# A message-passing kernel: when GpSimd may gather ahead, a step later for the first scatters, and where VectorE adds the biases

## The chip, the cores and the metric

One core of a Trainium2 chip. The metric is the device time of one execution in microseconds (us); lower is better. TensorE is called PE below, VectorE DVE, ScalarE ACT, GpSimd POOL and SyncE SP, as in the profile.

## The reference

25,000 edges, sorted by destination, join rows of `x` (100,000 nodes by 128, f32). Every edge makes a message, a gate weighs it, the messages are added up by destination, and each row of the result is normalised:

```python
src, tgt = (x[row], x[col])
h = jax.nn.relu(concatenate([src, tgt, edge_attr], axis=-1) @ W1 + b1)
msg = h @ W2 + b2
attn_weight = jax.nn.sigmoid(concatenate([msg, conf], axis=-1) @ Wa + ba)
out = segment_sum(msg * attn_weight, col, num_segments=N)
return layernorm(x + out)       # every one of the 100,000 rows
```

## The kernel before

The edges are worked off in 49 **steps** of 512 edges (four columns of 128). Sixteen steps are *near* steps (edges into the first 11,648 nodes, whose sums stay in SBUF in `near`), 33 are *list* steps (the other edges, whose rows are written one by one to `out`). `STEPS` fixes their order: list 0, list 1, near 15, list 2, list 3, near 14, then list 4 to 12 one after another (steps 6 to 14), near 13 (step 15), and from there mostly two list steps and a near one by turns. Beside the steps, 63 **chunks** of 1,408 plain rows of `x` are loaded, normalised and stored, three chunks for every two steps (one **batch**).

In a step k:

- POOL issues indirect DMAs, one for each column: four for the source rows (`gather_src`, into one of `RING` = 4 buffers of `rows_src`) and in a list step four more for the destination rows (`gather_dst`, into a ring of 4 `rows_dst` buffers that counts list steps alone; it waits for `stashed`, four list steps back). It also issues the **scatters** of finished list steps, four a list step, at the steps that `SCATTERS` names. All of these stand in one queue in program order.
- PE turns the three inputs (`turn(k)`: sources, destinations, attributes; each part raises `turned_ps_ready`), ACT copies them out, PE multiplies (`hidden(k)`), ACT applies relu, PE makes the messages (`messages(k)`, raises `msg_ready`).
- DVE adds the biases (`add_bias(k)`: a small `logit` and the raw messages `gated`, L1378 and L1381). ACT makes the gates and scales the messages (`gates(k)`).
- DVE adds the messages up, in a list step with `sum_list` (`acc`, then `stash`), in a near step with `sum_near` after PE placed them. At every even k DVE also runs `batch_scales`: a chain of 11 small dependent instructions (L1167 to L1178) with some normalising rows between them, ahead of it `near_stats` in some batches.

PE works off hidden(k), then placing or turning of sums (`sum_near`, `sum_head`, `turn_sums`), then turn(k+1), then messages(k). ACT works off relu(k), turn(k+1), rows of a chunk, gates(k), more rows. Both queues are in order, as DVE's is. At steps 13, 29 and 46 the PE queue has a `sum_head`, whose result DVE takes near the end of `sum_list` (L1330); a `turn_sums` in the same step (L959) waits until DVE has taken it (L1332), and turn(k+1) stands behind that.

What holds a gather back in the kernel before is `AHEAD` = 2: the gather of step k waits until PE has turned all three inputs of step k-2, although the ring has four buffers. The first scatters (list steps 0 and 1, at step 15) wait for the last plain chunk of their region to be stored and for the first part of `near` (`near_stored[0]`).

Of the kernel before, what the change touches and what calls it, by code (L numbers as in the profile page):

```python
# [14 lines left out]
G = 4  # L15
RING = 4
AHEAD = 2
SLOTS = 6
TRIO = 3
ROWS = 11  # L20
# [34 lines left out]
K = len(STEPS)  # L55
STEP_OF = {at: k for k, at in enumerate(STEPS)}

SCATTERS = {15: (0, 1), 18: (2, 3), 21: (4, 5), 24: (6, 7), 27: (8, 9), 29: (10,),
            32: (11, 12), 35: (13, 14), 38: (15, 16), 41: (17, 18), 44: (19, 20), 46: (21,),
            48: tuple(range(22, 33))}  # L60
STASH_G = 14
# [145 lines left out]
def build(nc, x, src, dstw, attr, conf, W1, b1, W2, b2, Wa, ba, out):  # L207
# [9 lines left out]
    with ExitStack() as ctx:  # L217
        def sb(name, shape, dt=F32):
            return ctx.enter_context(nc.sbuf_tensor(name, shape, dt))
# [4 lines left out]
        def sem(name):  # L224
            return ctx.enter_context(nc.semaphore(name))

        def sems(name, n):
            return [sem(f"{name}{i}") for i in range(n)]
# [45 lines left out]
        near = sb("near", [P, (NB + BEHIND) * F])  # L274
        nodes = sb("nodes", [P, SLOTS, ROWS, F])
        stats = sb("stats", [P, 2, WIDEST, STATS])
# [113 lines left out]
        near_landed = sem("near_landed")  # L390
        x_landed = sems("x_landed", SLOTS)
        turned_ps_ready = sem("turned_ps_ready")
# [19 lines left out]
        scale_free = sem("scale_free")  # L412
        normed = sems("normed", SLOTS)
        near_normed = sem("near_normed")
        stored = sems("stored", SLOTS)
        near_stored = sems("near_stored", len(NEAR_BATCHES))
# [46 lines left out]
        def chunk_parts(c):  # L463
            return REST_P if c == CHUNKS - 1 else P

        def chunk_of(view, c):
            n = chunk_parts(c)
            return view[ND + c * CHUNK:ND + c * CHUNK + n * ROWS].rearrange("(p r) f -> p r f", p=n)
# [15 lines left out]
        def table(t, i):  # L484

            return t[:, i // LG, (i % LG) * G:(i % LG) * G + G]
# [13 lines left out]
        def _(sp):  # L500
# [7 lines left out]
            def load_nodes(c):  # L508
                n = chunk_parts(c)
                sp.dma_start(nodes[0:n, c % SLOTS], chunk_of(x, c)).then_inc(x_landed[c % SLOTS], 16)  # L510

# [52 lines left out]
            def store_nodes(c):  # L564
                u, nth = c % SLOTS, c // SLOTS + 1
                n = chunk_parts(c)
                sp.wait_ge(normed[u], 2 * nth)
                sp.dma_start(chunk_of(out, c), nodes[0:n, u]).then_inc(stored[u], 16)
# [76 lines left out]
        def _(pool):  # L645
# [18 lines left out]

            def gather_src(k):
                kind, i = STEPS[k]
                if k >= AHEAD:

                    pool.wait_ge(turned_ps_ready, 3 * (k - AHEAD) + 3)
                idx = table(src_list, i) if kind == S_ else src_near[:, i * G:(i + 1) * G]  # L670
                for j in range(G):
                    pool.indirect_dma_start(  # L672
                        out=rows_src[:, k % RING, j, :], out_offset=None, in_=x[:, :],
                        in_offset=bass.IndirectOffsetOnAxis(ap=idx[:, j:j + 1], axis=0),
                    ).then_inc(src_got[k % RING], 16)
# [25 lines left out]
            for k in range(2, K):  # L701
# [3 lines left out]
                if is_list(k):  # L705
                    gather_dst(STEPS[k][1])
                for i in SCATTERS.get(k, ()):
                    if i in (0, 11, 22):
# [324 lines left out]
        def _(dve):  # L1033
            done = [0]

            def step(ins):
                done[0] += 1
                ins.then_inc(prep, 1)
# [227 lines left out]
            def near_norms(b):  # L1266

                assert not near_norm_rows(b)
                dve.wait_ge(scale_ready, 2 * (b + 1))
                dve.sem_inc(near_normed, 1)  # L1270
# [100 lines left out]
            def add_bias(k):  # L1371
                kind, i = STEPS[k]
                first = (LISTS * LT if kind == D_ else 0) + i * G

                dve.wait_ge(msg_ready, k + 1)
                if k == 0:
                    dve.wait_ge(lin_ready, 2)
                dve.tensor_tensor(logit[:, k % 2].rearrange("p (a b f) -> p a b f", a=2, b=2), msgs[:, :, :, F:F + 1],  # L1378
                                  lin[:, first:first + G].rearrange("p (a b f) -> p a b f", a=2, b=2), ALU.add
                                  ).then_inc(logit_ready, 1)  # L1380
                dve.tensor_tensor(gated[:, k % 2].rearrange("p (a b) f -> p a b f", a=2), msgs[:, :, :, 0:F],  # L1381
                                  b2_all[:, 0:F].unsqueeze(1).unsqueeze(1).to_broadcast([P, 2, 2, F]), ALU.add).then_inc(raw_ready, 1)
# [24 lines left out]
            for k in range(K + 3):  # L1407
                b = (k + 1) // 2
                if k % 2:
                    rows_now = norm_rows(b - 1, (0, 1)) + stat_rows(b, (0,))  # L1410
                else:
                    rows_now = stat_rows(b, (1, 2))
                if k == 2:
                    dve.wait_ge(fall_ps, 1)
                    step(dve.tensor_scalar(fell[:], sum_ps[:, 1, 300:301], 1.0, None, ALU.min))
                    settle()
                    step(dve.tensor_scalar(skip_all[:], fell[:], float(FAR), None, ALU.mult))
                    dve.tensor_copy(unsorted[:], fell[0:1, :]).then_inc(flag_ready, 1)
                    settle()
                    dve.wait_ge(list_ready, 1)  # L1420
                    dve.tensor_scalar(row_idx[:], row_idx[:], skip_all[:, 0:1], None, ALU.add).then_inc(list_ready, 1)
                spare = max(0, len(rows_now) - BESIDE)
                if is_list(k - 1):
                    do(rows_now[:spare])
                    sum_list(k - 1, rows_now[spare:])
                    list_stats(STEPS[k - 1][1], b)
                elif is_near(k - 1):
                    do(rows_now[:spare])
                    sum_near(k - 1, rows_now[spare:])
                else:  # L1430
                    do(rows_now)
                if k == V_STEP:
                    add_v()
                for piece in row_pieces_at(k):
                    add_rows(*piece)
                if is_near(k):
                    make_place(k)
                under = norm_rows(b - 1, (2,)) + near_norm_rows(b - 1) if k % 2 == 0 else []
                if b - 1 == BATCHES - 1:
                    near_norms(b - 1)  # L1440
                if (k % 2 == 0 or k == K) and b < BATCHES and k <= K:
                    if b in NEAR_OUT:
                        near_stats(b)
                    batch_scales(b, under)
                else:
                    do(under)
                if k < K:
                    add_bias(k)
                if is_near(k + 2) and k > 0:
                    make_pick(k + 2)  # L1450

# [91 lines left out]
```

## Time and profile before

| | |
|---|---|
| median of 3 runs | 635.19 us (630.9, 635.19, 635.46) |
| profiled execution | 633.0 us, span 631.2 us |
| busy | PE 394.6 us (63%), DVE 472.7 (75%), ACT 425.2 (67%), POOL 457.5 (72%) |
| DMA engines | 159.29 MB, mean 252 GB/s |
| mean granted PE clock | 0.825 |

The span runs from the first to the last instruction of the profiled execution; its own time is 1.8 us above its span. Busy time does not count waiting or issuing of DMAs by SP. An indirect DMA's row on POOL is the time in which POOL makes it up, not the time of its transfer.

### The profile page before, as it was taken

How to read it: one execution, taken by the hardware profiler on the slowest of the kernel's cores; microseconds unless marked ns; L12 is line 12 of the kernel's file. 1: busy time of each engine (PE TensorE's matmuls, PEld its weight loads, DVE VectorE, ACT ScalarE, POOL GpSimd, SP SyncE). 2: the span in 40 equal slices, each digit the busy share in tenths (PEclk: the TensorE clock that was granted, in tenths of full speed). 3: DMA queues.
4: the chain of work that ended last, by engine and by line, in shares of the span. 5: the costliest groups of instructions: out<-in, count | busy, mean ns of one | idle time of the engine just before them, and what ended most of it. 6: DMA issues, size and time to landing. Idle time of an engine off the chain costs nothing. (4 is left out here: it accounts for less than half of the span.)

```text
span 631.2 us, 7693 instructions
## 1 busy us (share of the span) xinstructions
PE 394.6 (63%) x1737; PEld 265.1 (42%) x1737; DVE 472.7 (75%) x1561; ACT 425.2 (67%) x1089; POOL 457.5 (72%) x473
## 2 busy tenths in 40 slices
PE   1694887765765749487575868486768667587100
PEld 0462544443543535255343545254445444365000
DVE  6899998989895888849688869989779759274200
ACT  0257798889784977677666968877985979247100
POOL 7575577777477777777777777777777777777772
PEclk9998987887786879778697989696898879598555
DMA  6977689898996898959879988999999768522210
GB/s 160 357 224 273 220 315 326 298 317 263 334 317 207 316 308 306 299 169 312 290 237 299 314 275 279 304 362 311 298 326 321 223 211 245 176 85 88 64 50 16
DMA packets 84529, 159.29 MB, mean 252 GB/s; under 512 B 14018, under 2 KB 54278, under 8 KB 84482
## 3 DMA queue, kind: packets, MB, share of 16 engines
q1 hardware_dynamic: 69762, 129.47, 60.4%
q0 software_dynamic: 14720, 29.32, 15.9%
q8 instruction: 14, 0.23, 0.1%
q14 instruction: 33, 0.27, 0.1%
HBM read 99.75 MB, written 59.95 MB: 253 GB/s over the span
## 5 line engine op out<-in xcount | busy, mean ns | idle before, releaser
L786 ACT ACTIVATE nodes<-nodes,sc 128x128 f32<-128x128 f32 (+1 forms) x462 | 184.0, 485 | 0.0
L689 POOL DMA_INDIRECT out<-stash,row_idx x132 | 135.0, 1023 | 47.3 <-issue 39.3
L672 POOL DMA_INDIRECT rows_src<-x,src_list x132 | 131.1, 993 | 51.3 <-issue 38.7
L914 PE MATMUL hid_ps<-turned,w 128*128 128x512 f32 x294 | 162.8, 697 | 4.1 <-ACT turned L767 4.0
L681 POOL DMA_INDIRECT rows_dst<-x,dst_list x132 | 127.7, 968 | 40.2 <-issue 39.9
L767 ACT ACTIVATE turned<-turn_ps 128x512 f32<-128x512 f32 x147 | 80.0, 588 | 95.9 <-PE turn_ps L888 48.0
L1186 DVE BATCH_NORM_STATS2 stats<-nodes 128x6 f32<-128x256 f32 (+1 forms) x358 | 133.6, 418 | 7.0 <-DMA nodes<-x 6.9
L924 PE MATMUL msg_ps<-w2x,hid 128*128 128x129 f32 x392 | 69.9, 335 | 47.3 <-ACT hid L772 47.3
L914 PEld LDWEIGHTS hid_ps<-turned,w 128*128 128x128 f32 x294 | 63.7, 233 | 69.0 <-issue 61.2
L924 PEld LDWEIGHTS msg_ps<-w2x,hid 128*128 128x128 f32 x392 | 63.2, 245 | 51.8 <-ACT hid L772 51.8
L672 POOL DMA_INDIRECT rows_src<-x,src_near x64 | 61.7, 965 | 22.3 <-issue 18.9
L1228 DVE TENSOR_SCALAR nodes<-nodes,sc 128x128 f32<-128x128 f32 (+1 forms) x231 | 70.6, 362 | 0.0
L782 ACT ACTIVATE gated<-gated,weight 128x128 f32<-128x128 f32 x196 | 62.6, 390 | 9.9 <-DVE gated L1381 6.7
L893 PE MATMUL turn_ps<-ident,rows_dst 128*128 128x128 f32 x132 | 27.1, 342 | 56.5 <-DMA rows_dst<-x,dst_list 56.5
L888 PE MATMUL turn_ps<-ident,rows_src 128*128 128x128 f32 x196 | 33.4, 298 | 37.7 <-DMA rows_src<-x,src_list 37.2
L786 ACT ACTIVATE stash<-stash,sc 128x128 f32<-128x128 f32 x132 | 53.9, 478 | 0.0
L949 PE MATMUL sum_ps<-place,gated 128*128 128x256 f32 (+3 forms) x128 | 44.0, 454 | 14.3 <-ACT gated L782 9.9
L1304 DVE SCALAR_TENSOR_TENSOR acc<-acc,keep,gated 128x128 f32<-128x128 f32 x129 | 43.8, 340 | 11.3 <-ACT gated L782 10.3
L1343 DVE TENSOR_TENSOR near<-near,sum_ps 128x256 f32 (+3 forms) x64 | 28.0, 437 | 28.9 <-PE sum_ps L949 28.1
L888 PEld LDWEIGHTS turn_ps<-ident,rows_src 128*128 128x128 f32 x196 | 25.3, 153 | 54.4 <-DMA rows_src<-x,src_list 44.2
L1378 DVE TENSOR_TENSOR logit<-msg_ps,lin 128x4 f32<-128x4 f32 x49 | 7.6, 156 | 53.1 <-PE msg_ps L924 53.1
L893 PEld LDWEIGHTS turn_ps<-ident,rows_dst 128*128 128x128 f32 x132 | 18.9, 173 | 61.3 <-DMA rows_dst<-x,dst_list 61.3
(129 smaller groups left out, 519.7 us busy)
## 6 DMA issues: line engine op xcount, KB each, us to landing
nodes<-x SPq DMA_DIRECT2D x62, 704.0 KB, 6.5
out<-nodes SPq DMA_DIRECT2D x62, 704.0 KB, 4.3
attr_in<-edge_attr SPq DMA_DIRECT2D x49, 256.0 KB, 5.2
near_dst<-line SPq DMA_DIRECT2D x16, 256.0 KB, 7.3
near_x<-x SPq DMA_DIRECT2D x20, 192.0 KB
near_x<-x SPq DMA_DIRECT2D x24, 128.0 KB
near<-x SPq DMA_DIRECT2D x4, 704.0 KB
out<-near SPq DMA_DIRECT2D x4, 704.0 KB, 7.5
```

Of the source, the lines that this page charges most:

```text
L672: pool.indirect_dma_start(out=rows_src[:, k % RING, j, :], out_offset=None, in_=x[:, :], in_offset=bass.IndirectOffsetOnAxis(ap=idx[:, j:j ...
L681: pool.indirect_dma_start(out=rows_dst[:, i % RING, j, :], out_offset=None, in_=x[:, :], in_offset=bass.IndirectOffsetOnAxis(ap=column(dst ...
L689: pool.indirect_dma_start(out=out[:, :], out_offset=bass.IndirectOffsetOnAxis(ap=column(row_idx, i, j), axis=0), in_=stash[:, list_slot(i) ...
L767: act.activation(turned[:, k % 2, c], turn_ps[:, c], ACT.Copy).then_inc(turned_ready, 1)
L782: act.activation(gated[:, k % 2, j, :], gated[:, k % 2, j, :], ACT.Copy, scale=weight[:, k % 2, j:j + 1]).then_inc(gated_ready, 1)
L786: return act.activation(row, row, ACT.Identity, scale=sc[0:parts, b % 2, 0, col:col + 1], bias=sc[0:parts, b % 2, 1, col:col + 1])
L888: last = pe.transpose(turn_ps[:, 0, j * P:(j + 1) * P], rows_src[:, s, j, :], ident[:])
L893: last = pe.transpose(turn_ps[:, 1, j * P:(j + 1) * P], rows_dst[:, i % RING, j, :], ident[:])
L914: last = pe.matmul(hid_ps[:], w1[:, c, :], turned[:, k % 2, c, :], start=(c == 0), stop=(c == 2))
L924: last = pe.matmul(msg(j), hid[:, k % 2, j * P:(j + 1) * P], w2x[:], start=True, stop=True)
L1186: return dve.bn_stats(st.rearrange("p w k -> p (w k)"), pair)
L1228: ins = dve.tensor_scalar(nodes[0:n, u, r, :], nodes[0:n, u, r, :], sc[0:n, b % 2, 0, col:col + 1], sc[0:n, b % 2, 1, col:col + 1], ALU.mu ...
```

## The change

Three edits, independent in the code:

1. `gather_src(k)` for k below `STARTING` = 12 waits for its buffer alone: nothing for k < 4, then the source part of turn(k-4). From step 12 on the wait is as before.
2. The scatters of list steps 0 and 1 stand behind the gathers of step 16, not 15.
3. DVE adds the biases of step k ahead of `near_stats` and `batch_scales`, not behind them.

```diff
+STARTING = 12
-SCATTERS = {15: (0, 1), 18: (2, 3), 21: (4, 5), 24: (6, 7), 27: (8, 9), 29: (10,),
+SCATTERS = {16: (0, 1), 18: (2, 3), 21: (4, 5), 24: (6, 7), 27: (8, 9), 29: (10,),
...
             def gather_src(k):
                 kind, i = STEPS[k]
-                if k >= AHEAD:
+                if k < STARTING:
+
+                    if k >= RING:
+                        pool.wait_ge(turned_ps_ready, 3 * (k - RING) + 1)
+                else:
 
                     pool.wait_ge(turned_ps_ready, 3 * (k - AHEAD) + 3)
...
                 if b - 1 == BATCHES - 1:
                     near_norms(b - 1)
+                if k < K:
+                    add_bias(k)
                 if (k % 2 == 0 or k == K) and b < BATCHES and k <= K:
                     if b in NEAR_OUT:
                         near_stats(b)
                     batch_scales(b, under)
                 else:
                     do(under)
-                if k < K:
-                    add_bias(k)
```

POOL around its first scatters, before (gathers of step 15, scatters, first gather of step 16):

```order
66 L672 DMA rows_src<-x,src_near 128x128 [waits turned_ps_ready]
67 L672 DMA rows_src<-x,src_near 128x128 x3
68 L689 DMA out<-stash,row_idx 100000x128 [waits stored5,stored4,list_ready,stored3,near_stored0,stored2,out_ready,stored1,stored0]
69 L689 DMA out<-stash,row_idx 100000x128 x3
70 L689 DMA out<-stash,row_idx 100000x128 [waits out_ready]
71 L689 DMA out<-stash,row_idx 100000x128 x3
72 L672 DMA rows_src<-x,src_list 128x128 [waits turned_ps_ready]
```

And in the changed kernel (line numbers are 5 higher there):

```order
65 L677 DMA rows_src<-x,src_near 128x128 [waits turned_ps_ready]
66 L677 DMA rows_src<-x,src_near 128x128 x3
67 L677 DMA rows_src<-x,src_list 128x128 [waits turned_ps_ready]
68 L677 DMA rows_src<-x,src_list 128x128 x3
69 L686 DMA rows_dst<-x,dst_list 128x128 [waits stashed]
70 L686 DMA rows_dst<-x,dst_list 128x128 x3
71 L694 DMA out<-stash,row_idx 100000x128 [waits stored5,stored4,list_ready,stored3,near_stored0,stored2,out_ready,stored1,stored0]
```

The gathers of step 16, with their wait for turn(14), moved ahead of the first scatters.

DVE at step 12, before (end of the chain of scales, biases, first row of the next sum):

```order
382 L1167 TENSOR_SCALAR sc_calc<-stats 128x42 [waits scale_free,stat_ready]
...
401 L1178 SCALAR_TENSOR_TENSOR sc<-stats,sc_calc 128x42
402 L1261 TENSOR_SCALAR near<-near,sc 128x128 x2
403 L1378 TENSOR_TENSOR logit<-msg_ps,lin 128x4 [waits msg_ready]
404 L1381 TENSOR_TENSOR gated<-msg_ps,b_all 128x512
405 L1228 TENSOR_SCALAR nodes<-nodes,sc 128x128 [waits scale_ready]
```

And in the changed kernel:

```order
382 L1383 TENSOR_TENSOR logit<-msg_ps,lin 128x4 [waits msg_ready]
383 L1386 TENSOR_TENSOR gated<-msg_ps,b_all 128x512
384 L1172 TENSOR_SCALAR sc_calc<-stats 128x42 [waits scale_free,stat_ready]
...
403 L1183 SCALAR_TENSOR_TENSOR sc<-stats,sc_calc 128x42
404 L1266 TENSOR_SCALAR near<-near,sc 128x128 x2
405 L1233 TENSOR_SCALAR nodes<-nodes,sc 128x128 [waits scale_ready]
```

The 21 rows of the chain now stand behind the wait for `msg_ready`; the same holds at every even step.

## Rows read from the trace of the kernel before

**Rows 1.** Page: busy time of the engines, and POOL's scatters (busy, mean ns; idle before).

```profile
PE 394.6 (63%) x1737; PEld 265.1 (42%) x1737; DVE 472.7 (75%) x1561; ACT 425.2 (67%) x1089; POOL 457.5 (72%) x473
...
L689 POOL DMA_INDIRECT out<-stash,row_idx x132 | 135.0, 1023 | 47.3 <-issue 39.3
```

**Rows 2.** Waits of POOL: total us, times, longest.

```profile
POOL rows_src L672 <- PE turn_ps L907: 15.1, 4, 9.3
POOL out L689 <- DMA out<-near: 7.4, 1, 7.4
```

**Rows 3.** Timeline of POOL: start, us, instruction, idle before it.

```profile
25.60 0.94 POOL L672 DMA_INDIRECT rows_src<-x,src_near  x1 [2.44 <-PE turn_ps L907]
...
67.60 0.94 POOL L672 DMA_INDIRECT rows_src<-x,src_list  x1 [9.27 <-PE turn_ps L907]
...
163.71 0.94 POOL L672 DMA_INDIRECT rows_src<-x,src_near  x1 [0.30 <-issue]
172.04 1.01 POOL L689 DMA_INDIRECT out<-stash,row_idx  x1 [7.39 <-DMA out<-near]
...
182.70 0.99 POOL L672 DMA_INDIRECT rows_src<-x,src_list  x1 [0.30 <-issue]
...
192.87 0.94 POOL L672 DMA_INDIRECT rows_src<-x,src_list  x1 [0.30 <-issue]
...
618.57 0.97 POOL L689 DMA_INDIRECT out<-stash,row_idx  x1 [0.30 <-issue]
```

**Rows 4.** Timeline of PE at step 13: sums turned, last part of turn(14).

```profile
168.60 0.55 PE L959 MATMUL sum_ps<-ident,near 128*128 128x128 f32 x3 [2.89 <-DVEq L1332]
...
169.86 0.60 PE L907 MATMUL turn_ps<-ident,attr_in 128*128 128x128 f32 x4
```

**Rows 5.** Waits of DVE between 60 and 156 us.

```profile
DVE acc L1304 <- ACT gated L782: 2.1, 4, 0.9
DVE logit L1378 <- PE msg_ps L924: 2.1, 2, 1.5
DVE near L1343 <- PE sum_ps L949: 1.7, 4, 0.8
DVE stats L1186 <- DMA nodes<-x: 0.7, 1, 0.7
```

**Rows 6.** Timeline of DVE at step 12: chain of scales, biases, next sum.

```profile
155.79 0.19 DVE L1167 TENSOR_SCALAR sc_calc<-stats 128x42 f32<-128x42 f32 x1
...
160.65 0.16 DVE L1378 TENSOR_TENSOR logit<-msg_ps,lin 128x4 f32<-128x4 f32 x1 [0.75 <-PE msg_ps L924]
...
161.32 1.64 DVE L1228 TENSOR_SCALAR nodes<-nodes,sc 128x128 f32<-128x128 f32 x6
163.67 0.36 DVE L1304 SCALAR_TENSOR_TENSOR acc<-acc,keep,gated 128x128 f32<-128x128 f32 x1 [0.70 <-ACT gated L782]
```

**Rows 7.** Timeline at step 11: DVE's logit, and ACT's gate that reads it.

```profile
148.80 0.14 DVE L1378 TENSOR_TENSOR logit<-msg_ps,lin 128x4 f32<-128x4 f32 x1
...
149.79 0.20 ACT L776 ACTIVATE weight<-logit 128x4 f32<-128x4 f32 x1
```

**Rows 8.** Timeline from turn(28) to the gathers of step 32, three engines.

```profile
345.31 1.11 PE L893 MATMUL turn_ps<-ident,rows_dst 128*128 128x128 f32 x4 [2.78 <-DMA rows_dst<-x,dst_list]
...
356.25 0.19 DVE L1167 TENSOR_SCALAR sc_calc<-stats 128x38 f32<-128x38 f32 x1
...
360.42 0.16 DVE L1378 TENSOR_TENSOR logit<-msg_ps,lin 128x4 f32<-128x4 f32 x1 [0.70 <-PE msg_ps L924]
...
364.38 0.35 DVE L1304 SCALAR_TENSOR_TENSOR acc<-acc,keep,gated 128x128 f32<-128x128 f32 x1 [1.66 <-ACT gated L782]
...
371.79 0.93 PE L907 MATMUL turn_ps<-ident,attr_in 128*128 128x128 f32 x4
...
373.00 0.94 POOL L672 DMA_INDIRECT rows_src<-x,src_near  x1 [0.94 <-PE turn_ps L907]
```

**Rows 9.** Timeline of DVE: the logit of step 44.

```profile
548.21 0.16 DVE L1378 TENSOR_TENSOR logit<-msg_ps,lin 128x4 f32<-128x4 f32 x1 [9.24 <-PE msg_ps L924]
```

## The prediction

> **What bounds the kernel now.** I read the page first. POOL's busy share of 72% looks harmless beside DVE's 75%, but its 460 indirect DMAs take 457.5 / 460 = 0.99 us each [rows 1] and between any two stands an issue gap of 0.30 us [rows 3]: 460 x (0.99 + 0.30) is some 594 us of a span of 631.2. The end is POOL's too: its last scatter starts at 618.57 [rows 3], DVE, ACT and PE have stopped before 600, and only landing and closing waits follow. So the second view is POOL's list of waits, and it is short [rows 2]: 15.1 us in four waits of source gathers for the third part of a turn, and 7.4 us in one wait of a scatter for the store of near rows. Less the 0.30 us that is there anyway, these are 2.1 us before step 2, 2.1 before step 3, 9.0 before step 6, 0.6 before step 32, and 7.1 before the first scatter: 20.9 us, of which 20.3 lie before 172 us. From the gather of step 17 (192.87) POOL works without a stop, but for the 0.6 us. The rule for the sum is therefore: the whole kernel moves by what the gather of step 17 moves, less any new wait behind it.
>
> **Edit 1 takes the first 13.2 us away from where they stand, and puts most of them elsewhere.** Steps 2, 3 and 6 start when POOL is free (their index tables are ready long before, and the buffers are untouched or turned). Then POOL reaches step 12 some 13 us early, where the old rule holds again: a gather waits for the turn two steps back. Destination gathers also wait for `stashed` four list steps back, which in steps 9 to 12 leaves POOL a lead of some 5 to 10 us, not 13. So the question is not how early POOL is but how early PE turns step 14, which the gather of step 16 needs. That turn ended at 169.86 + 0.60 = 170.46 [rows 4]. Ahead of it PE had waited 2.89 us, until 168.60, for DVE to take the head sum out of its bank, and DVE does that near the end of a sum whose first `acc` started at 163.67 [rows 6]. **DVE sets it.**
>
> How much faster can DVE be by then? Between 60 and 156 us it waited 2.1 + 2.1 + 1.7 + 0.7 = 6.6 us in 96 [rows 5]. It is 93% full with work in a fixed order. Before 60 us it hardly waits at all, so the early gathers buy nothing there. Of the 6.6 us I give back the waits that late data or late biases explain: 2.1 at the logits, and about half of the 3.8 at `acc` and `near`, together 3 to 5 us. ACT is no freer: at step 11 its gate came 1.0 us after DVE's logit [rows 7], so ACT cannot gain more than DVE by over 1 us.
>
> **Edit 3 moves the same 0.8 us of biases ahead of a chain of about 4 us.** What it does depends on whether the messages are there. Where DVE arrives late and they are there, ACT's gates start 3 to 4 us earlier. Where DVE arrives early, the chain used to fill the wait and now stands behind it. Step 12 is of the second kind [rows 6]: the chain began at 155.79, ran to 160.65 - 0.75 = 159.90, and the logit waited until 160.65 for the messages. In the changed order the chain (4.1 us) and the six rows (1.64) follow the biases (0.67), so the first `acc` stands 6.4 us behind the messages, where it stood 163.67 - 160.65 = 3.0 behind. The loss is 3.4 us, against what the messages gain. Let the messages of step 12 come d earlier; then the first `acc`, the head sum and turn(14) gain x = d - 3.4, if DVE itself is not later than that. With d at 5 to 6 (DVE's 3 to 5 plus up to 1 us), x is about 2. At the ends, d = 0 gives x = -3.4, and all of the waits of [rows 5] and 1 us more give x = +4.
>
> **Edit 2 takes the 7.1 us wait away.** The gather of step 16 used to start at 182.70, behind the scatters; now it starts at 170.46 + 0.30 - x. Its eight DMAs take until 192.87 - 0.30 in the old trace, 9.9 us, and then the two scatters (from 172.04 to 182.70 with the issue gap, 10.7) stand ahead of step 17. The near rows that they need were stored at 171.7, before 180, so that wait is gone and does not come back. Step 17 starts at 170.8 + 9.9 + 0.3 + 10.7 - x = 191.7 - x, against 192.87. Edits 1 and 2 together are worth 1.2 + x = 3.2 us, not 20: **a new wait of about 17 us at steps 12 to 16, for turns that DVE sets, takes the place of the old ones.** The gather of step 16 lands some 12 us earlier than it did, so PE and DVE catch up there; nothing on POOL's path uses it, since the next turns follow the gathers of step 17 again.
>
> **Behind step 17** compute mostly hangs on the data, so it moves with POOL. Where does compute hold POOL within a few us? I compared, for each step, the start of its source gather with the end of the turn two steps back. The least room is 0.3 us at step 32, then 1.9 to 4.9 at steps 18, 21, 24, 27, 35, 38, 41, 44 and 48, and in most of these the turn directly follows a landing, which moves along. Step 32 is different [rows 8]. Turn(28) ended a wait for the landing of its destination rows, so it is tied to POOL. From there DVE comes to its chain at 356.25 while the messages of step 28 come at 360.42. That wait grows from 0.70 to about 4.2 us under edit 3. After it stand biases 0.68, the chain (356.25 to 359.73, 3.5) and rows (1.6): `acc` at 366.2 instead of 364.38, 1.85 us later. PE's head sum waits for that, turn(30) ended at 371.79 + 0.93 = 372.72 and POOL's gather of step 32 already waited for it and started at 373.00. So **step 32 takes 1.85 us back.** Elsewhere the same loss at even steps fits in the room that I found.
>
> **The sum.** 1.2 + 2.0 - 1.85 = 1.4 us earlier. Against the profiled execution's own 633.0 us this is 631.6. The median of the three runs is 635.19, 2.2 above, so I say 633.8 for the median.
>
> One thing that would speak against the edit: does DVE slow POOL's issuing? An issue inside a stretch with DVE idle took 0.97 us at the end; over the whole kernel the scatters' mean is 1.02 [rows 1, 3]. So company of DVE costs about 0.05 us, and the 72 gathers of steps 2 to 11 at most 3.6 us, in a stretch where POOL will wait anyway: nothing. The Trainium skill, "SBUF — State Buffer", section "Who interferes with whom", says that VectorE in its two-port modes shuts GpSimd out for a whole instruction, copies and `tensor_scalar` among them. By that rule each of the 72 gathers could grow by the length of such a row, 0.27 us here (six in 1.64 us), 19 us in all, of which the new wait at steps 12 to 16 would swallow 17 and leave 2. The trace's mean speaks for a far smaller price.
>
> **Rivals.**
> - *Compute follows the gathers fully.* Then all of the waits come back (6.6 us up to 156, and some 1.5 at step 12), ACT's gates start early enough that the loss at steps 12 and 28 is hidden, and step 17 moves by 1.2 + 8.1 = 9.3 us: 635.2 - 9.3 = 626. For it: DVE, ACT and PE wait for each other in turns, and shortening one wait may cascade. Against it: at step 28 the messages hang on a landing and cannot gain. A partial form, x = 4 and no loss at step 32, gives 630.
> - *The chain behind the wait makes it slower.* The mechanism is that of steps 12 and 28, at every even step where DVE comes early. If the messages of step 12 gain nothing, 1.2 - 3.4 - 1.85 = -4.1, 639. It ends slower than before as soon as d is under about 4.1 us (1.2 + d - 3.4 - 1.85 < 0). At step 44 DVE waited 9.2 us for the messages even behind its chain [rows 9], so the whole chain comes on top there, some 3 us, against 3.4 us of room at step 48: if that is overrun by 2 to 3 us as well, 642. For it: such waits at even steps are common. Against it: most stand in stretches that POOL leads by far.
> - *The change doesn't bind at all.* If the early transfers crowd each other and the other loads of the start, gathers land later, d is only 2 to 4, and the result is 635 to 637 (1.2 + 3 - 3.4 - 1.85 = -1.1). This lies within the other cases' span.
>
> **Chances.** Forecast, 631 to 635.5: 0.5. Compute follows, 624 to 630.5: 0.22. Slower by the chain, 636 to 642: 0.22. Crowding: 0.06. A measurement of this kernel can tell about 1% (6.3 us) from no change; its own three runs lie 4.5 us apart. Faster by over 1% (under 628.8): 0.19. Slower by over 1% (over 641.5): 0.07. Within: 0.74. Range 627.5 to 640.
>
> **What would show it.** Right: POOL's waits before steps 2, 3 and 6 and before the first scatter are gone; a wait of 10 us or more for `turn_ps` L912 (L907 before) in front of steps 12 to 16, the largest at step 16; step 17 starts between 189 and 192 us; DVE's wait at the logit of steps 12 and 28 is 3 us or more; a wait of 2 to 3 us before step 32. Wrong: turn(14) ends before 164 us (compute follows, and DVE was not the bound), or step 32 does not wait, or new waits show at steps 20 to 31 or at step 48 (edit 3 costs more than I found room for). The forecast fails most easily in d, which I took from a sum of small waits.

## The result, and the profile after

| | before | after |
|---|---|---|
| median | 634.62 us (4 runs, 630.9 to 635.46) | 643.09 us (4 runs, 641.68 to 643.87) |
| ratio | 1 | 1.0141 [1.011, 1.0173] |
| profiled execution | 633.0, span 631.2 | 641.68, span 640.0 |

The changed kernel is 1.4% slower, 8.5 us. Line numbers after are 5 higher than before.

The page, busy times and POOL's scatters; they answer to [rows 1]: the counts are the same and the busy times nearly so (POOL's are 3.3 us up), but the span is 8.8 us longer.

```profile
PE 396.1 (62%) x1737; PEld 267.1 (42%) x1737; DVE 471.0 (74%) x1561; ACT 425.1 (66%) x1089; POOL 460.8 (72%) x473
...
L694 POOL DMA_INDIRECT out<-stash,row_idx x132 | 134.6, 1020 | 40.2 <-issue 39.6
```

POOL's waits after (total us, times, longest), beside [rows 2]:

```profile
POOL rows_src L677 <- PE turn_ps L912: 21.4, 4, 16.7
POOL rows_dst L686 <- DVE stash L1328: 7.2, 3, 6.2
```

POOL's timeline after, beside [rows 3] and the last line of [rows 8]:

```profile
159.42 0.94 POOL L677 DMA_INDIRECT rows_src<-x,src_near  x1 [0.30 <-issue]
177.09 0.94 POOL L677 DMA_INDIRECT rows_src<-x,src_list  x1 [16.73 <-PE turn_ps L912]
...
179.58 2.23 POOL L677 DMA_INDIRECT rows_src<-x,src_list  x1 [0.31 <-issue]
...
188.72 1.01 POOL L694 DMA_INDIRECT out<-stash,row_idx  x1 [0.30 <-issue]
...
199.20 0.99 POOL L677 DMA_INDIRECT rows_src<-x,src_list  x1 [0.30 <-issue]
...
381.47 0.94 POOL L677 DMA_INDIRECT rows_src<-x,src_near  x1 [2.74 <-PE turn_ps L912]
...
627.30 0.97 POOL L694 DMA_INDIRECT out<-stash,row_idx  x1 [0.30 <-issue]
```

The old waits are gone, and one of 16.73 us before step 16 stands in their place. The wait for the near store did not come back. The destination gathers also waited for `stashed`, 6.16 us at the longest, before 108.03; that took lead from POOL that it would otherwise have lost at step 16. Step 17 starts at 199.20 where it started at 192.87: 6.33 us later. At step 32 the lag is 381.47 - 373.00 = 8.47, and at the last scatter 627.30 - 618.57 = 8.73. So 6.3 us were lost before step 17, 2.1 by step 32, and 0.3 in all the rest. **In this pair of executions two places hold nearly the whole loss.**

The first place. PE's timeline at step 13 after, beside [rows 4]:

```profile
173.35 0.90 PE L964 MATMUL sum_ps<-ident,near 128*128 128x128 f32 x3 [6.05 <-DVEq L1337]
174.05 1.06 PE L893 MATMUL turn_ps<-ident,rows_src 128*128 128x128 f32 x4
...
175.75 1.06 PE L912 MATMUL turn_ps<-ident,attr_in 128*128 128x128 f32 x4
```

turn(14) ended at 175.75 + 1.06 = 176.81, not 170.46: 6.35 us later. 4.75 of them (173.35 against 168.60) are DVE's. The other 1.60 are PE's own: from the end of its wait to the end of turn(14) it needed 3.46 us where it had needed 1.86. The stretches around it, before and after, show why. A row gives the stretch and its length, the busy time of PE, of its weight loads, of DVE, ACT and POOL (instructions in brackets), then the granted clock, the DMA share and GB/s. Before:

```profile
165.00:168.00 3.00, 0.71 (x7) 0.47 (x5) 3.00 (x10) 1.55 (x4) 0.00 (x0) 1.00 1.02 366
168.00:171.00 3.00, 2.40 (x22) 2.40 (x23) 2.27 (x6) 1.38 (x3) 0.00 (x0) 1.00 1.06 335
```

After:

```profile
167.00:173.00 6.00, 0.30 (x3) 0.06 (x1) 5.97 (x22) 1.26 (x3) 0.00 (x0) 0.96 0.93 278
173.00:177.50 4.50, 4.15 (x20) 4.15 (x21) 2.06 (x5) 1.85 (x4) 0.41 (x1) 0.50 0.83 298
```

Before, PE idled 2.89 us and went on at a granted clock of 1.00 (2.4 GHz); after, it idled 6.05 us and went on at 0.50 (1.2 GHz), and the same four transposes took 1.06 us instead of 0.60. All the groups behind the wait follow each other at nearly twice the old distance, which accounts for the 1.60 us.

DVE's timeline at step 12 after, beside [rows 6]: logit, first and last row of the chain, rows, first `acc`.

```profile
162.35 0.16 DVE L1383 TENSOR_TENSOR logit<-msg_ps,lin 128x4 f32<-128x4 f32 x1 [4.52 <-PE msg_ps L929]
...
163.03 0.18 DVE L1172 TENSOR_SCALAR sc_calc<-stats 128x42 f32<-128x42 f32 x1
...
166.40 0.20 DVE L1183 SCALAR_TENSOR_TENSOR sc<-stats,sc_calc 128x42 f32<-128x42 f32 x1
...
167.03 1.61 DVE L1233 TENSOR_SCALAR nodes<-nodes,sc 128x128 f32<-128x128 f32 x6
168.56 0.34 DVE L1309 SCALAR_TENSOR_TENSOR acc<-acc,keep,gated 128x128 f32<-128x128 f32 x1
```

DVE stood idle for 4.52 us in front of a chain that had nothing to wait for. The first `acc` is 168.56 - 162.35 = 6.2 us behind the messages, where it was 3.0: the chain cost 3.2. And the messages themselves came 1.7 us later than before (162.35 against 160.65), not earlier. 3.2 + 1.7 = 4.9.

The waits of DVE between 60 and 156 us after, beside [rows 5]:

```profile
DVE logit L1383 <- PE msg_ps L929: 5.2, 5, 1.4
DVE stats L1191 <- DMA nodes<-x: 1.6, 2, 1.0
DVE near L1348 <- PE sum_ps L954: 1.2, 3, 0.6
```

8.0 us in place of 6.6. The waits at `acc` are gone, and waits at the logit took more than their place: 0.6 to 1.4 us at each of steps 4, 6, 8 and 10, with the chain behind them each time.

The second place. DVE at step 28 after, beside [rows 8]:

```profile
367.21 0.16 DVE L1383 TENSOR_TENSOR logit<-msg_ps,lin 128x4 f32<-128x4 f32 x1 [3.56 <-PE msg_ps L929]
...
373.04 0.34 DVE L1309 SCALAR_TENSOR_TENSOR acc<-acc,keep,gated 128x128 f32<-128x128 f32 x1
```

`acc` is 5.83 us behind the logit, where it was 364.38 - 360.42 = 3.96: 1.87 us more, and POOL's wait at step 32 grew from 0.94 to 2.74.

### The profile page after: what moved, and what is told of

Read it like the earlier page. It is cut to its first block and busy times, and to the rows that moved or that the text cites. A ratio compares the mean times of both kernels' runs of the same rounds, so it can differ in the third digit from the quotient of the medians.

```text
span 640.0 us, 7692 instructions
## 1 busy us (share of the span) xinstructions
PE 396.1 (62%) x1737; PEld 267.1 (42%) x1737; DVE 471.0 (74%) x1561; ACT 425.1 (66%) x1089; POOL 460.8 (72%) x473
## 5 line engine op out<-in xcount | busy, mean ns | idle before, releaser
L677 POOL DMA_INDIRECT rows_src<-x,src_list x132 | 135.3, 1025 | 58.0 <-issue 38.4
L919 PE MATMUL hid_ps<-turned,w 128*128 128x512 f32 x294 | 159.3, 684 | 4.4 <-ACT turned L772 4.3
L919 PEld LDWEIGHTS hid_ps<-turned,w 128*128 128x128 f32 x294 | 61.9, 226 | 68.2 <-issue 59.9
L954 PE MATMUL sum_ps<-place,gated 128*128 128x256 f32 (+3 forms) x128 | 48.4, 501 | 28.2 <-DVE near L1348 14.5
L898 PE MATMUL turn_ps<-ident,rows_dst 128*128 128x128 f32 x132 | 25.5, 326 | 39.9 <-DMA rows_dst<-x,dst_list 39.9
L954 PEld LDWEIGHTS sum_ps<-place,gated 128*128 128x128 f32 x128 | 24.2, 221 | 54.7 <-DVE near L1348 28.9
L907 PE MATMUL turn_ps<-pick,near_x 128*128 128x128 f32 x280 | 38.1, 295 | 10.1 <-DVE pick L1361 10.1
L893 PEld LDWEIGHTS turn_ps<-ident,rows_src 128*128 128x128 f32 x196 | 26.8, 158 | 38.5 <-DMA rows_src<-x,src_list 26.0
```

The lines of the kernel that those rows point to most:

```text
L677: pool.indirect_dma_start(out=rows_src[:, k % RING, j, :], out_offset=None, in_=x[:, :], in_offset=bass.IndirectOffsetOnAxis(ap=idx[:, j:j ...
L893: last = pe.transpose(turn_ps[:, 0, j * P:(j + 1) * P], rows_src[:, s, j, :], ident[:])
L919: last = pe.matmul(hid_ps[:], w1[:, c, :], turned[:, k % 2, c, :], start=(c == 0), stop=(c == 2))
L954: pe.matmul(sum_ps[:, use % 2, 0:width * P], gated[:, k % 2, j, :], place[:, b * P:(b + width) * P], start=True, stop=True).then_inc(sum_r ...
```

## The experiments

The first theory after the result: edit 3 makes DVE late through waits at the even steps, and the early gathers give nothing back. The rival: the early gathers or the moved scatters crowd the transfers and do the harm. The edits are independent, so each was run alone and in pairs.

**Edit 3 alone** (edits 1 and 2 left out).

The edit, against the kernel before:

```diff
+                if k < K:
+                    add_bias(k)
                 if (k % 2 == 0 or k == K) and b < BATCHES and k <= K:
...
-                if k < K:
-                    add_bias(k)
```

> Edit 3 alone (biases ahead of the chain of scales at every step; gathers and scatters as before). Theory A, the chain behind the wait for messages makes VectorE late: turn(14) ends 5 to 7 us later than 170.5, the near rows are stored as much later, the first scatter starts near 179 us and not 172.0, step 32 adds 2 us; the kernel is slower by 7 to 9 us, 641 to 644. Theory B, the early gathers crowd or collide with something and edit 3 is harmless: the time is that of before, 633 to 636. Theory C, edit 3 costs only in company with the gathers (its losses need the turn of step 14 on GpSimd's path): turn(14) is late but the time stays at 635 to 637.

638.36 us, 1.0087 [1.0047, 1.0128]. PE at step 13, for which the row of before is in [rows 4]:

```profile
171.19 0.90 PE L959 MATMUL sum_ps<-ident,near 128*128 128x128 f32 x3 [5.90 <-DVEq L1332]
...
173.59 0.85 PE L907 MATMUL turn_ps<-ident,attr_in 128*128 128x128 f32 x4
```

turn(14) ended at 174.44, 4.0 us later. But step 17 started at 193.1, 0.2 later: without edit 2, turn(14) doesn't stand on POOL's path, since POOL waits for the near store and then has its scatters to issue. That store was not late either: the first scatter started at 171.58, where the expectation had 179. What is left is step 32, whose gather waits 2.9 us and comes 3.1 later (376.1 against 373.0): most of the 3.5 us by which this execution's span (634.7) is longer. The medians lie 6.8 apart; the other half of that stands in no trace, and the profiled execution is the fastest of the four. The time falls between theories A and C. Edit 3 costs by itself, clear of the noise.

**Edits 1 and 2 together** (edit 3 left out; the edit is against the changed kernel).

```diff
-                if k < K:
-                    add_bias(k)
                 if (k % 2 == 0 or k == K) and b < BATCHES and k <= K:
...
+                if k < K:
+                    add_bias(k)
```

> Edits 1 and 2 without edit 3. Theory A: VectorE keeps its chain in the wait, turn(14) ends 2 to 4 us earlier than 170.5, step 17 starts 3 to 5 us earlier than 192.9 and step 32 takes nothing: 630 to 632. Theory B: the early gathers are what costs, so this is as slow as the changed kernel, 641 to 644.

633.56 us, 1.0004 [0.9959, 1.0049]. POOL's gather of step 16 came at 172.65 behind a wait of 13.67, step 17 at 193.81: 20 us of waits removed, and step 17 one microsecond *later*. The 630 to 632 of theory A did not come, and theory B (641 or more) is out. DVE's waits from 60 to 156 us, and SP's (the queue that loads and stores plain rows; L511 is its wait for a buffer to be stored, L569 its wait for rows to be normalised):

```profile
DVE stats L1191 <- DMA nodes<-x: 5.7, 3, 2.2
DVE near L1348 <- PE sum_ps L954: 1.0, 2, 0.8
DVE acc L1309 <- ACT gated L787: 0.3, 1, 0.3
DVE logit L1383 <- PE msg_ps L929: 0.2, 1, 0.2
...
SPq L511 <- DMA out<-nodes: 39.7, 12, 6.9
SPq L569 <- ACT nodes L791: 34.0, 10, 5.8
```

This is where d went. The early gathers did take DVE's waits at `acc` and the logit away (4.2 us to 0.5), as predicted. But DVE then reached the plain rows earlier than these were loaded, and waited there: 5.7 us in place of 0.7. The total is 7.2 against 6.6. The exchange shows in every kernel with the chain first. In the four with edit 1 (edits 1, 2; edit 1; and, below, edit 3 from step 16 and edits 1, 2 with PE's order changed) the waits at `acc` and the logit are 0.5 us and those for plain rows 3.1 to 5.7; in the four without it (before; edit 2; and, below, PE's order changed alone and with edit 2) they are 3.4 to 4.3 and 0 to 0.7. The loads of plain rows did not come earlier: SP issued two of them from 155.90 before and from 156.36 here. Its loads wait for stores, and the stores for rows that ACT and DVE normalise.

**Edit 1 alone**, with `SCATTERS` as before and the biases behind.

> Edit 1 alone. The first scatters still wait at step 15 for the store of the near rows, which VectorE sets. Theory A: the lead of GpSimd ends there, the wait grows from 7 to about 18 us, and the gain is what VectorE gains by then, 0 to 4 us: 631 to 635. Theory B: 640 or more.

633.25 us, 1.0008 [0.9958, 1.0058]. POOL's waits:

```profile
POOL out L694 <- DMA out<-near: 13.5, 1, 13.5
POOL rows_src L677 <- PE turn_ps L912: 4.0, 2, 2.3
POOL rows_dst L686 <- DVE stash L1328: 2.8, 1, 2.8
```

The scatter that waits for the near store started at 171.03, 1.0 us earlier than before. Its wait grew by 6.1 us, to 13.5 and not to the 18 expected, since other new waits stand ahead of it: 2.8 us for `stashed` and 1.7 for a turn. (The other wait for a turn, 2.3 us, is that of step 32.) Of the 13 us that edit 1 had won, step 17 kept 0.3.

**Edit 2 alone** (`SCATTERS = {16: (0, 1), ...` in the kernel before, and nothing else).

> Edit 2 alone. Gathers of step 16 start after turn(14) at 170.8 us, step 17 at about 191.7 and not 192.9: 1.2 us faster, 633 to 635, by both theories. If it is slower than before, the wait for turn(14) costs more than the wait for the near rows that it replaces.

633.57 us, 1.002 [0.9971, 1.007]. The wait for the near store went, a wait of 10.2 us at step 6 stayed, and step 17 came at 193.0: the gather of step 16 started 0.3 us behind turn(14) at 171.0, and its eight DMAs took 11.3 us where I had reckoned with 9.9. That eats the 1.2 us of edit 2 at step 17.

**Edits 2 and 3**, without the early gathers.

> Edits 2 and 3 without edit 1. Theory A (edit 3 delays turn(14), and edit 2 puts turn(14) on GpSimd's path): turn(14) ends near 174 to 176 us as with edit 3 alone, the gather of step 16 starts with it, step 17 starts at 196 to 198 us instead of 192.9, and step 32 adds 3: 640 to 643, nearly as slow as the whole change although the gathers start as before. Theory B (the early gathers carry the loss beyond edit 3's own): 636 to 639.

643.7 us, 1.0143 [1.0102, 1.0185]: the whole loss of the change. PE at step 13:

```profile
174.59 0.90 PE L959 MATMUL sum_ps<-ident,near 128*128 128x128 f32 x3 [6.77 <-DVEq L1332]
...
176.99 1.06 PE L907 MATMUL turn_ps<-ident,attr_in 128*128 128x128 f32 x4
```

Step 17 started at 200.1, later than the 196 to 198 expected; this execution is the slowest of its four. So edit 1 does no harm and no good. Edit 3 makes turn(14) late, and edit 2, harmless alone, takes away the scatters that covered it. At step 17 this is plain: 0.2 us later with edit 3 alone, 0.1 with edit 2 alone, 7.3 with both. The times (0.9% and 0.2% alone, 1.4% in a pair) agree, but their intervals are too wide to show by themselves that the pair costs more than the sum.

**Edit 3 for one half of the steps**, with edits 1 and 2: for k below 16, and for k from 16 on. Odd steps have no chain and are the same in both.

```diff
+def bias_first(k):
+    return k % 2 or k < 16
...
+                if k < K and bias_first(k):
+                    add_bias(k)
...
+                if k < K and not bias_first(k):
+                    add_bias(k)
```

> All three edits, but the biases go ahead of the chain only up to step 15. Theory A: step 17 starts near 199 us as in the changed kernel, and the gather of step 32 waits no longer than it does without edit 3 (about 2 us): 639 to 641, i.e. two thirds of the loss are made by step 16. If the loss comes from edit 3 at all of the later steps: 634 to 636.

> All three edits, but the biases go ahead of the chain only from step 16 on. Theory A: step 17 starts at 193 to 194 us, the gather of step 32 waits 3 to 5 us for turn(30): 636 to 638. If early steps make no loss: 641 to 643.

Below 16: 639.8 us, 1.0095 [1.0064, 1.0126]; step 17 at 198.4. From 16: 635.98 us, 1.0021 [0.9987, 1.0054]; step 17 at 190.4, earlier than the 193 to 194 expected, but with a wait of 3.5 us at step 32. The first half carries most of the loss, as POOL's timeline said; what the second half costs is not clear of the noise.

The kernel with edit 3 from step 16 on is, up to turn(14), the same as edits 1 and 2 alone, yet it ended turn(14) at 168.7 and the other at 172.4. One execution is a loose gauge of this place, and it is better to read all of them:

| profiled executions | logit of step 12 | end of turn(14) |
|---|---|---|
| chain first: before; edit 2; edit 1; edits 1, 2; from 16 | 160.6; 160.5; 159.9; 161.1; 158.9 | 170.5; 170.7; 169.7; 172.4; 168.7 |
| biases first: edit 3; edits 2, 3; below 16; all three | 160.2; 163.6; 161.6; 162.4 | 174.4; 178.1; 176.1; 176.8 |

The means are 170.4 and 176.3: **edit 3 costs 6.0 us at turn(14)**. With or without the early gathers the means are 170.3 (edit 1; edits 1, 2; from 16) and 170.6 (before; edit 2): **edit 1 brings 0.3 us there**, and 0.6 at the logit of step 12 (160.0 against 160.6), both within the spread.

The same goes for the wait at step 32. With edit 3 at step 28 and PE's order as before it is 2.7, 2.9, 4.3 and 3.5 us; without it 0.9, 0.6, 2.3, 2.2, 2.3 (below 16) and 0.9 (the next kernel). The means are 3.3 and 1.5, so edit 3 costs some 1.8 us there, but a single execution can be 1 us off either way.

**Biases first only where the traces showed DVE late for them** (edits 1 and 2 as in the change).

```diff
+def bias_first(k):
+    return k % 2 or k in (0, 10, 14, 30, 38)
```

> Edits 1 and 2, and of the even steps only 0, 10, 14, 30 and 38 have the biases ahead of the chain: there the messages had come before VectorE was ready in the kernel before. Theory A (only the chain behind a wait costs): no loss at step 12 or 28, 630 to 634, as without edit 3. If biases ahead of the chain cost by making the next sum late even without a wait: 636 or more.

633.77 us, 0.9998 [0.997, 1.0027]. No loss, and no gain that shows: earlier gates at these five steps moved nothing on POOL's path.

**PE's order at the head sums.** If PE's wait for DVE is what holds turn(14), the turn can stand ahead of it: nothing in turn(14) needs the head sum. Only the order in PE's queue at steps 13 and 29 is changed, on top of edits 1 and 2.

```diff
+                first = k in (HEAD_STEP[0], HEAD_STEP[1])
+                if first:
+                    turn(k + 1)
                 for piece in row_pieces_at(k):
                     turn_sums(*piece)
-                if k + 1 < K:
+                if k + 1 < K and not first:
                     turn(k + 1)
```

> Edits 1 and 2 without edit 3, and at steps 13 and 29 TensorE turns the next step's inputs ahead of turning the near sums, so that turn(14) and turn(30) no longer stand behind VectorE's taking of the head sum. Theory A (that queue place is what holds GpSimd): turn(14) ends near 167 us instead of 172, step 17 starts near 189, the wait at step 32 is gone: 625 to 628. If VectorE's pace alone holds turn(14), whatever the order on TensorE: 632 to 635.

626.86 us, 0.9895 [0.9854, 0.9937], the first version that beats both kernels. PE at step 13, and POOL's first gathers of steps 16 and 17:

```profile
165.33 0.60 PE L912 MATMUL turn_ps<-ident,attr_in 128*128 128x128 f32 x4
165.77 0.60 PE L964 MATMUL sum_ps<-ident,near 128*128 128x128 f32 x4
168.27 0.55 PE L964 MATMUL sum_ps<-ident,near 128*128 128x128 f32 x3 [1.90 <-DVEq L1340]
...
166.20 1.05 POOL L677 DMA_INDIRECT rows_src<-x,src_list  x1 [8.24 <-DMA out<-nodes]
...
187.72 0.99 POOL L677 DMA_INDIRECT rows_src<-x,src_list  x1 [0.30 <-issue]
```

PE still waits for DVE, but behind turn(14), which now ends at 165.93. Step 17 starts at 187.7, 5.2 us earlier than before, and the wait at step 32 is gone (0.30). The gather's named releaser is a store, but it starts 0.27 us behind turn(14), as in the other traces with edit 2 (0.27 or 0.28), and the program lets it wait for nothing but the turn: the turn released it.

**The whole change with this order, and this order on the kernel before.**

> The whole change and, at steps 13 and 29, TensorE's turn of the next step ahead of turning the near sums. Theory A (edit 3's loss reaches GpSimd only through the head sum that turn(14) and turn(30) stand behind): turn(14) ends near 168 us instead of 177, step 17 starts near 190, step 32 does not wait: 628 to 632, where the whole change takes 643. If edit 3 costs wherever it makes VectorE late: 638 or more.

> The kernel before with TensorE's order alone changed at steps 13 and 29. GpSimd's first scatters still wait for the near rows at 172 us, so only the 0.6 us at step 32 can come back: 632 to 635. If turn(14) held more than the trace of before shows: under 630.

The first: 630.08 us, 0.9929 [0.9905, 0.9953], against 1.0141 without the order and 0.9895 without edit 3. The second: 633.56 us, 0.9991 [0.9967, 1.0016], although its turn(14) ended at 166.75. Its POOL waits say why:

```profile
POOL rows_src L672 <- PE turn_ps L907: 14.5, 3, 10.0
POOL out L689 <- DMA out<-near: 8.3, 1, 8.3
```

The scatters ahead of step 16 wait for the near store until 173.15. The early turn pays only where edit 2 has moved the scatters behind it.

**DVE's work taken away.** The prediction held that DVE, 93% full, sets turn(14). This kernel (edits 1 and 2) leaves out part of the computation: DVE normalises only one row of each plain chunk in the first seven batches, some 13 us of work less.

```diff
+                if b < 7 and r != ROWS - 1:
+                    return
```

(The biases stand behind the chain, as in edits 1 and 2.)

> Edits 1 and 2, and VectorE leaves out all but one of its normalising rows of every plain chunk in the first seven batches (about 8 rows of 0.27 us a batch, some 13 us by step 13); those rows of the output are left unnormalised. Theory A (VectorE's work sets turn(14), the gathers have a lead to spare): turn(14) ends 6 to 13 us earlier than 172. If GpSimd's gathers or ScalarE set it: 2 us or less.

632.01 us in one run. turn(14) ended at 169.7, inside the range of the full kernels (168.7 to 172.4). DVE's waits from 60 to 156 us:

```profile
DVE stats L1191 <- DMA nodes<-x: 6.8, 3, 5.2
DVE acc L1311 <- ACT gated L787: 4.3, 5, 2.0
DVE near L1350 <- PE sum_ps L954: 3.7, 4, 1.5
DVE logit L1385 <- PE msg_ps L929: 0.7, 1, 0.7
```

15.5 us of waits in place of 7.2: the freed time turned into waits for ACT, PE and the loads. My theory fell here: it wanted turn(14) 6 to 13 us earlier. DVE is full, but its amount of work alone doesn't set turn(14).

**Is it ACT, then, or the stores?** Three kernels on edits 1 and 2 leave out work: ACT's normalising rows but one a chunk in the first seven batches; both engines' rows; all but one of 11 stored rows of the first 21 chunks. A fourth is edit 2 with PE's order, without edit 1.

> Edits 1 and 2, and ScalarE leaves out all but one of its normalising rows of each plain chunk in the first seven batches (some 19 rows of 0.4 us a batch, about 7 us for every two steps); the rows are left unnormalised. If ScalarE's work paces the first stage: turn(14) ends over 8 us earlier than 172. If VectorE's work and ScalarE's pace it in turn: 2 to 6 us. If neither: under 2.

> As light_scalar, and VectorE leaves out its normalising rows too (as in light_vector). If the two engines together pace the stage: turn(14) ends 12 us or more earlier than 172, up to where GpSimd's own gathers set it (gathers of step 14 would end near 139 without a wait). If the stores and reloads of the chunks pace it: no more than 3 us earlier than with light_scalar.

> Edits 1 and 2, and the first 21 plain chunks store one of their eleven rows (the rest of those rows of the output is left unwritten), which takes about 14 MB from the DMA engines and lets the reloads start earlier. If the chunk loop through memory paces the stage: VectorE's waits for node loads go and turn(14) ends 4 us or more earlier than 172. If the engines do: under 2.

> Edit 2 and TensorE's turn ahead of the near sums at steps 13 and 29, with the gathers held as before (no edit 1, no edit 3). If the earlier gathers are worth nothing even here: step 17 starts near 189 us and the time is that of turn_first, 625 to 629. If edit 1 is what lets the turn come early: 630 to 633.

All four ran on a chip where the kernel before itself took 759.39 us, with waits ahead of POOL's gathers that no other trace of this study has (60.1 us in 32 waits in the fourth), so the times of the first three (771.93, 750.93 and 769.94 us) say nothing about this case. The fourth took 754.18 us, a ratio of 0.9856 [0.9712, 0.9999] to the kernel before on the same chip. Two of the four were run again elsewhere. The kernel with both engines lighter has DVE's lines from above and, for ACT:

```diff
-                for r in range(ACT_ROWS[i]):
+                for r in range(ACT_ROWS[i] - 1 if b < 7 else 0, ACT_ROWS[i]):
```

> Edits 1 and 2, and VectorE and ScalarE both leave out all but one of their normalising rows of each plain chunk in the first seven batches; the rows are left unnormalised. If the two engines' work in turns paces the first stage: turn(14) ends 12 us or more earlier than 172 us. If the stores and reloads of chunks or the chain of a step itself pace it: 5 us or less.

623.18 us in one run, beside 635.26. PE at step 13:

```profile
161.71 1.06 PE L912 MATMUL turn_ps<-ident,attr_in 128*128 128x128 f32 x4
```

DVE's and ACT's waits from 60 to 156 us:

```profile
DVE stats L1191 <- DMA nodes<-x: 1.4, 1, 1.4
...
ACT weight L781 <- DVE logit L1385: 27.9, 9, 8.3
```

With both engines lighter turn(14) ended at 162.8, 5.9 us below the earliest full kernel of this order and 9 below the 172 of the expectation, between its two cases (12 or more, 5 or less). Step 17 started at 184.4, and the loads kept DVE waiting for only 1.4 us. So the work of DVE and ACT together moves turn(14), where DVE's alone did not. It is one execution, and PE still waited 4.92 us for DVE ahead of that turn. Whether the two act through the gates that they hand each other or through the plain rows that both must finish before a buffer is stored and loaded again is not shown: ACT alone and the stores alone were not measured on a chip that tells.

> Edit 2 and TensorE's turn ahead of the near sums at steps 13 and 29; gathers held as before. If the earlier gathers are worth nothing even here: step 17 starts near 189 us and the time is that of turn_first, 0.985 to 0.993 of before. If edit 1 is what lets the turn come early: 0.994 or more.

Edit 2 and PE's order, gathers as before: 626.86 us, 0.9895 [0.9849, 0.9941], the same ratio as with edit 1. **Even where the turn comes early, edit 1 brings nothing that shows**: turn(14) ended at 166.0 here and 165.9 there, step 17 started at 187.2 and 187.7.

## Why the prediction was wrong

It said 633.8 us, 627.5 to 640, with 0.07 for slower by over 1%. It is 643.09.

- *POOL's issuing is the bound, and everything moves with step 17.* Right. 6.33 us at step 17 and 2.1 at step 32 give 8.5 of the 8.8 us of the span. In every complete kernel above the span moved as the gather of step 32 did, within 1.9 us.
- *The old waits go and a wait of about 17 us takes their place.* Right: 16.73 us before step 16.
- *Edit 2 is worth 1.2 us.* Right in form, off in size: it also assumed that the gathers of step 16 take 9.9 us. They took 11.3 after (one of them 2.23 instead of 0.94) and 11.3 with edit 2 alone. From the first gather of step 16 to that of step 17 passed 22.1 us in place of the 20.9 of the sum. With this, edit 2 alone is worth nothing.
- *Edit 3 moves the chain behind the wait at step 12, at a price of 3.4 us.* Right: 3.2, and in edit 3 alone as well. At step 28 it was 1.87 against a predicted 1.85; so close a hit is in part luck, given how the waits at step 32 scatter, but their means differ by 1.8 too.
- ***"Let the messages of step 12 come d earlier", with d of 5 to 6.* This is the step that failed.** The runs show 0.6 from edit 1 without edit 3, which is within the spread, and with all three edits the messages came 1.7 us *later*. I had added up DVE's waits and given back those that late data explained. They did go away, and waits for plain rows took their place: a wait that one input gives back belongs to the next input that is late. The table of waits shows the last of several, and I hadn't asked what is second.
- *The lower bound of x, -3.4, at d = 0.* Too narrow, since x came out at -6.35. This step failed as well. I took for granted that edit 3 could do harm only at step 12. The waits at steps 4 to 10, which I had seen as "common" and passed over as "in stretches that POOL leads", stand ahead of work of DVE's that turn(14) waits for: the mean logit of step 12 is 161.9 in the four kernels with edit 3 of the table, against 160.2. PE's order at step 13 cannot reach that logit, so the kernels with PE's order changed count too; with them the means are 162.1 of five (160.2 to 163.6) and 160.2 of eight (158.9 to 161.1). In edit 3 alone, though, it came at 160.2, so this delay is loosely measured, and that the waits at steps 4 to 10 make it is argued and not shown by a run of its own. And PE's transposes behind the longer wait ran at the lower clock: from the end of the wait to the end of turn(14) the four kernels with edit 3 took 3.4 us and the five without 2.2. On the means: 1.7 + 3.2 + 1.2 = 6.1, of 6.0 measured.
- *"DVE sets it."* Half right: DVE's lateness sets it in edit 3, but relieving DVE alone gained nothing that shows.
- *The rival "the chain behind the wait makes it slower"* is what happened, with its mechanism and its place; its price was 639. The difference is what the last two points name: with x = -6.35 and 1.2 for the slower gathers of step 16 the same sum gives 1.2 - 6.35 - 1.2 - 1.85 = -8.2, against 8.5 in the medians. Its second part, an overrun at step 48, did not happen.
- *The rival "compute follows the gathers fully"* is out: with edits 1 and 2 and no edit 3 it wanted over 9 us, and the ratio is 1.0004. The time came down only when PE's order was changed too.
- *Crowding of the issues.* Small, as predicted. In the stretch 20 to 120 us after, with the early gathers in it, POOL's rows read

```profile
L677 POOL DMA_INDIRECT rows_src<-x,src_list x32 | 33.3, 1041 | 9.7 <-issue 9.4 <-PE turn_ps L912 0.3
```

  against a mean of 985 ns for 29 of them before. The 0.06 us between the means is a single gather, which took 2.84 us at 30.80: (2.84 - 0.94) / 32 = 0.06. DVE was busy for 90% of this stretch after, and 34 of the 40 source gathers in it took 0.94 to 0.99 us. The Trainium skill, "SBUF — State Buffer", section "Who interferes with whom", says that VectorE's two-port instructions shut GpSimd out for a whole instruction. By that each gather could have grown by up to 0.27 us, an estimate from the length of such a row here. The trace does not bear that out for the issuing of gathers.

## What to carry to other kernels

Before you move an instruction that waits ahead of work that doesn't, look at the wait and not at the instruction: in an in-order queue everything behind it is late by as much as the wait grows. The gain, if any, is to move a wait *behind* what others need, as PE's turn ahead of its wait for DVE showed (1.4% lost by the whole change, 1% won by that order with edit 2). When you give back a wait, name the input that is late next, with its own row, before you book the gain. And a cover that one edit removes (the scatters ahead of step 16) can make another edit's harmless delay count in full, so pairs have to be priced, not only single edits.

## What was not expected of the hardware

PE's clock added to a stall that it didn't cause: behind 2.89 us of idling it was granted 1.00, behind 6.05 us 0.50. In edits 1 and 2 alone it was granted 0.61 in the mean of the 4.1 us behind 4.31 us of idling, so both levels stood in that stretch. In edit 2 alone, behind 3.48 us, it went on at 1.00 for 1.2 us and then at 0.54. In edit 3 alone and in edits 2 and 3 the transposes of the source rows behind the wait took 1.06 us in place of 0.60.

Now and then POOL needs up to 2.8 us to make up an indirect DMA where most take 0.94. This doesn't need a wait of POOL's: the gather of 2.84 us at 30.80 follows others at 0.30 us, and the 150th indirect DMA after took 2.53 us, at 220.75, without one. The slow ones come at nearly the same places in POOL's queue in every kernel: all 16 kernels traced on chips where the kernel before takes 631 to 636 us have one of 1.36 us or more among its 148th to 152nd, its 175th to 178th and its 203rd to 206th indirect DMA. With edit 2 one falls among the gathers of step 16. The cause was not looked for.
